# A recurrent scan on one core: expert products in half-precision parts, smaller blocks, a shorter lead and another order on VectorE

## Chip, core and metric

One Trainium2 chip, one of its cores. The metric is the device time of one execution in microseconds (us). TensorE (PE) has two clock levels, 1.2 and 2.4 GHz; a profile shows the granted one as a share of 2.4 GHz.

## What is computed

Four layers on x of shape 8 x 256 x 512. The change touches layer 1's expert part and layer 2's wide product, and the order of work in the scan that computes layers 1 and 2 together:

```python
# layer 1, conditioning: a GRU over 256 steps, state h of 8 x 512
r = sigmoid(i_r + h_r); z = sigmoid(i_z + h_z); n = tanh(i_n + r * h_n)
h = (1 - z) * n + z * h
# layer 1, experts, on every state h of the GRU
base_out = einsum('bsd,od->bso', x, W_base) + b_base
expert_idx = argmax(softmax(x @ router_W.T)); onehot = one_hot(expert_idx)
out = base_out + 2 * einsum('bser,eor->bso', (x @ A) * onehot, Bw)
# layer 2, conditioning: 256 Runge-Kutta steps (4 evaluations each)
dq = q - q**3/3 - p + drive + tanh(q) @ coupling.T + bias     # drive = layer 1's output at that step
dp = 0.08 * (q + 0.7 - 0.8 * p)
# layer 2, retrieval: hidden layer of 2048 on every state q
h = silu(q @ W_up.T + b_up);  h = h @ W_down.T + b_down        # then keys, top 8, gather by products
```

## The kernel before

Phases run one after the other, each closed by a barrier of all engines: attention and experts of layer 0, gates (`gates`, the GRU's input products), `scan`, `retrieve_experts`, attention and experts of layer 3.

**The scan.** The GRU runs LEAD = 29 steps ahead of the oscillator (the Runge-Kutta steps), since the drive of oscillator step t is the expert output for GRU state t. So there is a prologue of 29 GRU steps alone (first `for s in range(LEAD)` of every engine), then the loop over t = 0 to 255 in which oscillator step t and GRU step s = t + 29 are woven together, and from t = 227 on the oscillator is alone. Nothing plans the order: it is written out by hand for every engine, and each engine runs its list in order, with semaphores between them.

- *TensorE.* One evaluation k = 0..3 of a step (`evaluate`) is 16 products of 8 columns (L631, low part of the weights) and 16 of 16 columns (L634, high part with both parts of the state), all 128x128 f16 weights. Between evaluations lie the GRU's three gates R, N and Z in the same form (`gate_low`, `gate_high`), 96 products a step. At the end of a step comes a slice of the experts (`experts`), for blocks of TL = 16 steps, 128 columns of states, in f32: slices 0 and 1 the router and A product (L663), 2 to 9 the base product (L669), slice 4 also a transpose (L672), 10 and 11 the product with Bw (L676). So 12 of 16 steps carry a slice. In a profile an f32 product counts as two matmul records.
- *VectorE.* It sums the partial products (L863, "reduce" below; it ends each evaluation), makes the low part of tanh(q) for TensorE (`low_part`, L852), and the cubic term, the Runge-Kutta sums and the GRU's elementwise work. Its order in evaluation 0 is: G0 and Q, Z gate's first sum (`pre`, L763 into g_a), `low_part`, `arg`, cubic, Q1, `total`, then the GRU update (`upd`, `state_half` L802, `state_full` L806), then the reduce. After evaluation 3's reduce comes the clamp (L867). In slice 12 it adds bias and x to the expert output (L826, four instructions of 128x128) into XT.
- *ScalarE.* tanh(q) twice (L723 as f16, L724 as f32), the scaled copies (L726, L709), square, the gates' sigmoids and tanh.
- *GpSimd (POOL).* Per step the drive (L745, L747), L752, and the copy of q into HQ (L756).

**Retrieval.** For s = 0..7 (256 tokens each) TensorE runs `up` (L1006: 16 tiles m by 4 chunks, f32 weights 128x128, 256 columns, two PSUM banks in turn), `pairs`, `similar`, `down`; ScalarE empties the banks (`hidden`, L1108), VectorE does top 8. The weights wait in GRZ, loaded by DMA once the GRU has ended.

Of the kernel before, what the change touches and what calls it, by code (L numbers as in the profile page):

```python
# [573 lines left out]
LEAD, TL = 29, 16  # L574

def scan(nc, K, XT, GRZ, HQ, wm, whi, wlo, chi, clo, bhn, cond_d, bias_d, wb_d, bb_d, ar_d, bw_d, wup, wdn, wup_d, wdn_d, s_pw):

    with ExitStack() as c:
# [49 lines left out]
        def _(e):  # L628
# [1065 lines left out]
```

## Time and profile before

| | us |
|---|---|
| median of 3 runs | 5070.73 (5060.59 to 5075.04) |
| profiled execution | 5060.11 |
| its span | 5058.5 |
| TensorE busy | 4811.2 (95%) |
| VectorE busy | 2748.1 (54%) |
| ScalarE busy | 1687.5 (33%) |
| GpSimd busy | 357.5 (7%) |
| mean granted TensorE clock | 0.781 |

The scan takes the stretch from about 903 to 2899 us of the span, retrieval from 2901 to 4310. A busy share counts an instruction's whole duration, so overlapping ends of pipelined matmuls hide short gaps: in the scan a step is read better from the start times of its groups.

### The profile page before, as it was taken

What the parts mean: (1) busy time and instruction counts of PE and PEld (TensorE: products, weight loads), DVE (VectorE), ACT (ScalarE), POOL (GpSimd) and SP (SyncE); (2) the same over time, 40 slices, a digit from 0 to 9 for tenths busy, and PEclk for the clock granted to TensorE, in tenths of its full rate; (3) what the DMA queues carried; (4) which work ended last, traced back from release to release, by engine and by line L of the source; (5) the groups of instructions that cost most, each with busy time, mean ns of one, the idle gap of its engine ahead of it and who ended that gap; (6) DMA issues with size and microseconds to landing.
All of it is one profiled execution on the core that took longest, in us unless ns stands there. A gap on an engine that the chain in (4) does not pass through costs nothing. (4 is left out here: it accounts for less than half of the span.)

```text
span 5058.5 us, 197415 instructions
## 1 busy us (share of the span) xinstructions
PE 4811.2 (95%) x83680; PEld 3821.2 (76%) x83680; DVE 2748.1 (54%) x15134; ACT 1687.5 (33%) x7030; POOL 357.5 (7%) x1123
## 2 busy tenths in 40 slices
PE   8999989699999999999998699999999999999999
PEld 3335654699999999999997588789999999444444
DVE  3110020488888888888888726575553342344421
ACT  1101111245555555555554322233322221233320
POOL 1100010011111111111111100000000000000000
PEclk7999989555555555555555599999989999899999
DMA  3202330000000000000001000023320000100000
GB/s 106 106 10 111 150 124 8 16 4 5 5 5 5 5 5 5 5 5 5 5 5 53 13 9 2 33 71 94 92 77 3 3 3 2 47 8 8 10 7 33
DMA packets 52292, 159.62 MB, mean 32 GB/s; under 512 B 13873, under 2 KB 14001, under 8 KB 46272
## 3 DMA queue, kind: packets, MB, share of 16 engines
q1 hardware_dynamic: 45408, 130.70, 7.7%
q8 instruction: 651, 10.67, 0.9%
q0 software_dynamic: 3712, 12.29, 0.7%
q10 hardware_dynamic: 2304, 4.20, 0.2%
q14 instruction: 217, 1.78, 0.1%
HBM read 129.63 MB, written 17.17 MB: 29 GB/s over the span
## 5 line engine op out<-in xcount | busy, mean ns | idle before, releaser
L631 PE MATMUL k_ps<-k_hx,k_wlo 128*128 128x8 f16 x16384 | 604.9, 169 | 95.5 <-ACT k_hx L723 95.0
L631 PEld LDWEIGHTS k_ps<-k_hx,k_wlo 128*128 128x128 f16 x16384 | 545.7, 105 | 135.2 <-ACT k_hx L723 111.0
L634 PE MATMUL k_ps<-k_hl,k_whi 128*128 128x16 f16 x16384 | 590.0, 174 | 2.9 <-issue 0.4
L634 PEld LDWEIGHTS k_ps<-k_hl,k_whi 128*128 128x128 f16 x16384 | 519.4, 104 | 7.4 <-issue 1.8
L631 PE MATMUL g_ps<-g_hx,g_wlo 128*128 128x8 f16 x12288 | 434.2, 168 | 47.1 <-DVE g_hx L802 41.9
L634 PE MATMUL g_ps<-g_hl,g_whi 128*128 128x16 f16 x12288 | 436.9, 174 | 4.2 <-issue 4.1
L631 PEld LDWEIGHTS g_ps<-g_hx,g_wlo 128*128 128x128 f16 x12288 | 384.9, 104 | 59.0 <-DVE g_hx L802 52.3
L634 PEld LDWEIGHTS g_ps<-g_hl,g_whi 128*128 128x128 f16 x12288 | 385.1, 104 | 4.4 <-issue 4.4
L723 ACT ACTIVATE k_hx<-k_q 128x32 f16<-128x32 f32 x768 | 176.1, 229 | 567.1 <-DVE k_q L863 564.1
L1475 DVE TENSOR_REDUCE t_NM<-t_ps 128x1 f32<-128x512 f32 x256 | 165.0, 686 | 218.3 <-PE t_ps L1341 218.3
L863 DVE TENSOR_REDUCE k_q<-k_ps 128x32 f32<-128x96 f32 x768 | 196.8, 256 | 147.6 <-PE k_ps L634 122.0
L1246 DVE TENSOR_TENSOR HQ<-p_ior,p_pm 128x2048 f32<-128x2048 f32 x61 | 139.4, 2290 | 217.0 <-PE p_sim L1065 217.0
L490 DVE TENSOR_TENSOR m_hT<-GRZ,m_ps 128x256 f32<-128x256 f32 (+1 forms) x72 | 36.6, 508 | 383.5 <-ACT GRZ L453 377.4
L1075 PE MATMUL p_dn<-wm,GRZ 128*128 128x128 f32 x2048 | 241.4, 280 | 2.0 <-ACT wm L1133 2.0
L1075 PEld LDWEIGHTS p_dn<-wm,GRZ 128*128 128x128 f32 x2048 | 235.3, 195 | 3.4 <-ACT wm L1133 2.2
L1075 PE MATMUL p_pq<-r_mem,GRZ 128*128 128x128 f32 x2048 | 236.3, 276 | 0.0
L726 ACT ACTIVATE k_hl<-k_hx 128x32 f16<-128x32 f16 x1024 | 235.1, 230 | 0.0
L1075 PEld LDWEIGHTS p_pq<-r_mem,GRZ 128*128 128x128 f32 x2048 | 230.9, 192 | 1.1
L1006 PE MATMUL p_up<-HQ,GRZ 128*128 128x256 f32 x1024 | 225.2, 382 | 1.8 <-PEq L22 1.8
L1006 PEld LDWEIGHTS p_up<-HQ,GRZ 128*128 128x128 f32 x1024 | 196.5, 192 | 29.1 <-issue 1.9
L728 ACT ACTIVATE k_sq<-k_q 128x32 f32<-128x32 f32 x1024 | 218.1, 213 | 0.0
L852 DVE CUSTOM_DVE_ANT_0 k_hl<-k_T,k_hx 128x32 f16<-128x32 f32 x1024 | 191.1, 187 | 7.9 <-ACT k_T L724 0.2
(340 smaller groups left out, 8994.4 us busy)
## 6 DMA issues: line engine op xcount, KB each, us to landing
GRZ<-expert_places SPq DMA_DIRECT2D x64, 512.0 KB, 4.9
wm<-in_w_dram SPq DMA_DIRECT2D x4, 2816.0 KB, 10.2
GRZ<-in_w_dram SPq DMA_DIRECT2D x4, 2816.0 KB, 9.8
m_w<-in_w2a_dram SPq DMA_DIRECT2D x8, 1280.0 KB, 12.6
GRZ<-in_ue_dram SPq DMA_DIRECT2D x8, 1024.0 KB, 7.9
GRZ<-in_x_nat_dram SPq DMA_DIRECT2D x4, 1024.0 KB, 10.3
XT<-in_xT_dram SPq DMA_DIRECT2D x1, 4096.0 KB, 26.9
expert_rows<-wm SPq DMA_DIRECT2D x1, 4096.0 KB, 17.3
```

The costliest lines, as they stand in the source:

```text
L490: V.tensor_tensor(hT[0:M,m,0:n],sA[0:M,st,0:n],ps[st*2+1][0:M,0:n],ALU.mult).then_inc(s_h,1)
L631: T.matmul(P[:,1,j*NB:(j+1)*NB],lo[:,kc,(m0+j)*128:(m0+j+1)*128],x[:,kc,:],start=(j==0 and kc==0),stop=False,skip_group_check=True)
L634: i=T.matmul(P[:,:,j*NB:(j+1)*NB],hi[:,kc,(m0+j)*128:(m0+j+1)*128],x[:,kc,:,:],start=False,stop=kc==KC-1,skip_group_check=True)
L723: A.activation(kx[:],m4(src),ACT.Tanh,scale=uq[k]).then_inc(k_hi,1)
L726: A.activation(kl[:,:,0,:],kx[:],ACT.Copy,scale=S).then_inc(k_hS,1)
L728: A.activation(sq[:],q[:,k,:],ACT.Square,scale=uq[k]).then_inc(k_sq,1)
L852: V.tensor_tensor_reduce(kl[:,:,1,:],m4(Tt[:]),kx[:],S,0.0,ALU.subtract,ALU.max,lz[:,0:1]).then_inc(k_lo,1)
L863: V.tensor_reduce(qn[:] if k==3 else q[:,k+1,:],ksum(k),AX.X,ALU.add).then_inc(k_q,1)
L1006: x=T.matmul(psu[n%2][:,(m%2)*256:(m%2+1)*256],wup[:,dd,m*128:(m+1)*128],HQ[:,dd,s*256:(s+1)*256],start=dd==0,stop=dd==3)
L1075: x=T.matmul(pso[i%2][:,dd*128:(dd+1)*128],ue[:,cc,dd*128:(dd+1)*128],Ws[i%2][:,cc,:],start=cc==0 and dd==0,stop=cc==31,skip_group_check=True)
L1246: V.tensor_tensor(B0[q] if i==0 else Bp[:,q],bc(ior[:].unsqueeze(1),[128,16,128]),bc(PM[:,i,1,q*16:(q+1)*16].unsqueeze(2),[128,16,128]),AL ...
L1475: V.tensor_reduce(NM[:,qc,hh*64+32:hh*64+33],psX[hh][:,:],AX.X,ALU.max,negate=True).then_inc(s_mx,1)
```

## The change

1. Experts of the scan in f16: the weights (base and A with router) are scaled and split on GpSimd into a high and a low f16 part; each f32 product becomes three f16 products (high x high, high x low, low x high). The states are kept as f16 parts (HX, HL) written by the GRU's own instructions, in place of HS; the f32 state stays in HF for two steps. The product with Bw stays f32.
2. Blocks of TL = 8 steps (64 columns); slices at steps 0 to 6 of 8. LEAD = 17.
3. Expert output: ScalarE copies PSUM to `ex` (slice 7), GpSimd adds it to XT; the bias is added to XT beforehand on GpSimd. VectorE's four instructions (L826) are gone.
4. VectorE's order: the Z gate's `pre` and `arg` and the clamp (`limit`) come ahead of `low_part(t,0)`, then `diff` (before ahead of evaluation 3's reduce), G0, Q, `upd`, cubic, `state_half`, `total`, reduce; `state_full` and Q1 move into evaluation 1; `low_part` goes ahead of `low` and of `pre(s,R)` in evaluations 1 and 2.
5. q goes to HQ as two f16 parts: GpSimd runs three instructions a step (`state_out`) in place of one copy.
6. Retrieval's `up`: W_up is split into f16 parts at the start of the phase, in four rounds of one ScalarE copy and one VectorE instruction, 128x2048 each, and each product becomes three f16 products of 256 columns.

```diff
-LEAD, TL = 29, 16
+LEAD, TL = 17, 8
 # TensorE, experts
+                def base(u0,u1):
+                    for u in range(u0,u1):
+                        dc,d=u//4,u%4
+                        P=pso[:,dc*TN:(dc+1)*TN]; wh=wbh[:,d,dc*128:(dc+1)*128]; wl=wbl[:,d,dc*128:(dc+1)*128]
+                        T.matmul(P,wh,hS[:,d,:],start=u==0,stop=False,skip_group_check=True)
+                        T.matmul(P,wh,lS[:,d,:],start=False,stop=False,skip_group_check=True)
+                        T.matmul(P,wl,hx[:,d,:],start=False,stop=False,skip_group_check=True)
...
-                    for d in (2*i,2*i+1):
-                        x=T.matmul(psh[:,0:136],hs[:,d,:],ar[:,d,:],start=d==0,stop=d==3)
+                    for d in (2*i,2*i+1):
+                        T.matmul(psh[0:TN,0:136],hS[:,d,:],arh[:,d,:],start=d==0,stop=False)
+                        T.matmul(psh[0:TN,0:136],lS[:,d,:],arh[:,d,:],start=False,stop=False)
+                        x=T.matmul(psh[0:TN,0:136],hx[:,d,:],arl[:,d,:],start=False,stop=d==3)
+                    base(i,i+1)
+                if i==2: base(2,7)
+                if i==3:
+                    base(7,11)
+                    e.wait_ge(l_ht,j+1)
+                    T.transpose(pst[:,0:TN],ht[:],K.ident[0:TN,0:TN]).then_inc(l_tr,1)
+                if i==4: base(11,16)
+                if i in (5,6):
 # ScalarE, evaluation 1
+            def expert_out(s):
+                if i!=7 or j<0 or j>=NT//TL: return
+                e.wait_ge(l_o,j+1)
+                if j>0: e.wait_ge(l_x,j)
+                A.activation(ex[:].rearrange('p d t b -> p (d t b)'),pso[:,0:KC*TN],ACT.Copy,scale=US).then_inc(l_e,1)
 # GpSimd, ahead of its loop
+            e.wait_ge(s_lw,64)
+            G.tensor_scalar(both,both,SW,None,ALU.mult).then_inc(s_sp,1)
+            G.tensor_copy(high,both).then_inc(s_sp,1)
+            G.tensor_tensor(both,both,high,ALU.subtract).then_inc(s_sp,1)
+            G.tensor_scalar(low_,both,S,None,ALU.mult).then_inc(s_sp,1)
+            for dc in range(KC): G.tensor_scalar(XT[:,dc],XT[:,dc],bb[:,dc:dc+1],None,ALU.add).then_inc(s_bx,1)
 # GpSimd, in its loop
-                    G.tensor_copy(HQ[:,:,:,t-1],m4(q[:,0,:])).then_inc(k_out,1)
+                    state_out(t-1)
+                results(t+LEAD)
 # VectorE, evaluation 0
+                if t>0:
+                    pre(s-1,Z_)
+                    limit(t-1)
+                    arg(s-1,Z_)
+                low_part(t,0)
+                if t>0: diff(s-1)
                 e.wait_ge(k_q0,t+1)
                 n_G=ch.did(stt(G0[:],p[:],-BETA*6/h,q[:,0,:]))
                 e.wait_ge(k_u,t+1)
                 n_Q=ch.did(stt(Q[:,0,:],q[:,0,:],1/3,E0[:]))
-                if t>0: pre(s-1,Z_)
-                low_part(t,0)
-                if t>0: arg(s-1,Z_)
+                if t>0: upd(s-1)
                 cubic(t,0)
-                n_Q1=ch.did(stt(Q[:,1,:],G0[:],-a*EPS*h/6,Q[:,0,:]))
+                if t>0: state_half(s-1)
                 total(t,0,Q[:,0,:],n_Q)
-                if t>0: upd(s-1); state_half(s-1); state_full(s-1)
                 end(t,0)
+                if t>0: state_full(s-1)
 # retrieval
-                        x=T.matmul(psu[n%2][:,(m%2)*256:(m%2+1)*256],wup[:,dd,m*128:(m+1)*128],HQ[:,dd,s*256:(s+1)*256],start=dd==0,stop=dd==3)
+                        T.matmul(P,wh,qh,start=dd==0,stop=False)
+                        T.matmul(P,wh,ql,start=False,stop=False)
+                        x=T.matmul(P,wl,qh,start=False,stop=dd==3)
...
+            for x in range(4):
+                if x>0: e.wait_ge(s_wl,x)
+                A.activation(wpair(x)[:,:,0,:],wup[:,:,x*512:(x+1)*512],ACT.Copy,scale=SW).then_inc(s_wh,1)
...
+            for x in range(4):
+                e.wait_ge(s_wh,x+1)
+                V.scalar_tensor_tensor(wpair(x)[:,:,1,:],wup[:,:,x*512:(x+1)*512],SW,wpair(x)[:,:,0,:],ALU.mult,ALU.subtract).then_inc(s_wl,1)
```

## Rows read from the trace of the kernel before

**Rows 1.** Busy time by stretch: from:to, length, PE, PEld, DVE, ACT, POOL, clock, DMA.

```profile
1033.00:2700.00 1667.00, 1624.84 (x51403) 1584.93 (x51404) 1450.52 (x11206) 843.09 (x5224) 222.45 (x904) 0.50 0.02 5
...
3040.00:3240.00 200.00, 197.03 (x924) 160.19 (x923) 119.05 (x743) 54.97 (x104) 0.00 (x0) 1.00 0.01 2
```

**Rows 2.** PE timeline, a step without experts: start, us, engine, line, count, idle before.

```profile
1268.14 0.59 PE L631 MATMUL k_ps<-k_hx,k_wlo 128*128 128x8 f16 x16 [0.25 <-ACT k_hx L723]
1268.75 0.57 PE L634 MATMUL k_ps<-k_hl,k_whi 128*128 128x16 f16 x16
...
1270.15 0.57 PE L631 MATMUL k_ps<-k_hx,k_wlo 128*128 128x8 f16 x16
1270.58 0.57 PE L634 MATMUL k_ps<-k_hl,k_whi 128*128 128x16 f16 x16
...
1271.77 0.59 PE L631 MATMUL k_ps<-k_hx,k_wlo 128*128 128x8 f16 x16
...
1273.92 0.57 PE L634 MATMUL k_ps<-k_hl,k_whi 128*128 128x16 f16 x16
...
1275.18 0.59 PE L631 MATMUL k_ps<-k_hx,k_wlo 128*128 128x8 f16 x16 [0.25 <-ACT k_hx L723]
```

**Rows 3.** PE timeline, a step that ends with an expert slice.

```profile
1244.78 1.20 PE L669 MATMUL l_pso<-g_HS,wm 128*128 128x128 f32 x4
1245.77 0.61 PE L631 MATMUL k_ps<-k_hx,k_wlo 128*128 128x8 f16 x16
...
1253.07 0.61 PE L631 MATMUL k_ps<-k_hx,k_wlo 128*128 128x8 f16 x16
```

**Rows 4.** Timeline of all engines from one step's last reduce to evaluation 0's.

```profile
1046.68 0.25 DVE L863 TENSOR_REDUCE k_qn<-k_ps 128x32 f32<-128x96 f32 x1
...
1047.36 0.24 POOL L756 COPY HQ<-k_q 128x32 f32<-128x32 f32 x1
...
1047.53 0.18 DVE L852 CUSTOM_DVE_ANT_0 k_hl<-k_T,k_hx 128x32 f16<-128x32 f32 x1
...
1048.35 0.19 DVE L802 TENSOR_TENSOR g_hx<-g_m,g_n 128x32 f16<-128x32 f32 x1
...
1048.56 0.25 DVE L863 TENSOR_REDUCE k_q<-k_ps 128x32 f32<-128x96 f32 x1
```

**Rows 5.** Bounds of the scan's stages: two prologue steps, the oscillator's first and last, t = 227, L826.

```profile
942.19 1.02 PE L631 MATMUL g_ps<-g_hx,g_wlo 128*128 128x8 f16 x32 [1.58 <-DVE g_hx L802]
...
946.50 1.01 PE L631 MATMUL g_ps<-g_hx,g_wlo 128*128 128x8 f16 x32 [1.58 <-DVE g_hx L802]
...
L631 PE MATMUL k_ps<-k_hx,k_wlo x16384: 167/168/214, 1033.4 to 2898.4; 128*128 128x8 f16 x200
...
2704.05 0.59 PE L631 MATMUL k_ps<-k_hx,k_wlo 128*128 128x8 f16 x16 [0.25 <-ACT k_hx L723]
...
1264.50 1.46 DVE L826 SCALAR_TENSOR_TENSOR XT<-l_pso,l_bb,XT 128x128 f32<-128x128 f32 x4
```

**Rows 6.** PE timeline of retrieval, `up` of two rounds.

```profile
3047.36 27.79 PE L1006 MATMUL p_up<-HQ,GRZ 128*128 128x256 f32 x128
...
3097.68 12.68 PE L1006 MATMUL p_up<-HQ,GRZ 128*128 128x256 f32 x58
```

**Rows 7.** Groups by line and shape: engine, shapes, count, busy us, mean ns, idle before.

```profile
L459 ACT ACTIVATE GRZ<-m_ps 128x512 f32<-128x512 f32 x8 | 4.7, 592 | 0.0
...
L568 DVE SCALAR_TENSOR_TENSOR g_wc<-g_wc,g_whi 128x2048 f32<-128x2048 f32 x3 | 6.9, 2292 | 0.1
...
L1108 ACT ACT_TABLE_LOAD x13 | 16.7, 1283 | 9.3 <-PE p_up L1006 9.1
```

**Rows 8.** GpSimd prices, and a VectorE instruction beside one of GpSimd's in layer 0.

```profile
L225 POOL MEMSET a_RS<- 128x1024 f32 x1 | 1.0, 951 | 0.0
...
29.63 4.50 POOL L231 TENSOR_TENSOR a_wor<-a_wor 16x2048 f32<-16x2048 f32 x1
32.73 1.68 DVE L246 TENSOR_SCALAR a_CB<-a_cm,a_pc 128x512 f32<-128x512 f32 x1
```

More of the change, by code:

```diff
@@ L640, in gate_low @@
                 if x==R_ and j0==0: e.wait_ge(g_hi,s+1)
-                for j in range(j0,j1): products_low(gsum(x),wlo,hx,x*4,j)
+                for j in range(j0,j1): products_low(gsum(x),wlo,hxs(s),x*4,j)
             def gate_high(s,x,j0,j1):
@@ L644, in gate_high @@
                 if x==R_ and j0==0: e.wait_ge(g_lo,s+1)
-                for j in range(j0,j1): i=products_high(gsum(x),whi,hl,x*4,j)
+                for j in range(j0,j1): i=products_high(gsum(x),whi,lambda kc: hls(s)[:,:,kc,:],x*4,j)
                 if j1==KC: i.then_inc(g_mm[x],1)
@@ L651, in evaluate @@
                 e.wait_ge(k_lo,t*4+k+1)
-                for j in range(KC): i=products_high(kout[k%2],chi,kl,0,j)
+                for j in range(KC): i=products_high(kout[k%2],chi,lambda kc: kl[:,kc,:,:],0,j)
                 i.then_inc(k_mm,1)
@@ L735, in _ @@
                         scaled(s)
-                    elif k==1: masked(s)
+                    elif k==1: masked(s); expert_out(s)
                     elif k==2: sig_r(s)
@@ L747, in drive, with results, state_out @@
                 G.tensor_scalar(Ds[:],D[:],1/US,None,ALU.mult).then_inc(k_Ds,1)
+            def results(s):
+                j,i=s//TL-1,s%TL
+                if i!=7 or j<0 or j>=NT//TL: return
+                e.wait_ge(l_e,j+1)
+                x=XT[:,:,:,j*TL:(j+1)*TL].rearrange('p d b t -> p d t b')
+                G.tensor_tensor(x,ex[:],x,ALU.add).then_inc(l_x,1)
+            e.wait_ge(s_lw,64)
+            both=wm[:,0:2592]; high,low_=split[:,0:2592],split[:,2592:5184]
+            G.tensor_scalar(both,both,SW,None,ALU.mult).then_inc(s_sp,1)
+            e.wait_ge(s_sp,1)
+            G.tensor_copy(high,both).then_inc(s_sp,1)
+            e.wait_ge(s_sp,2)
+            G.tensor_tensor(both,both,high,ALU.subtract).then_inc(s_sp,1)
+            e.wait_ge(s_sp,3)
+            G.tensor_scalar(low_,both,S,None,ALU.mult).then_inc(s_sp,1)
+            for dc in range(KC): G.tensor_scalar(XT[:,dc],XT[:,dc],bb[:,dc:dc+1],None,ALU.add).then_inc(s_bx,1)
+            def state_out(t):
+                if t>0: e.wait_ge(k_ol,t)
+                G.tensor_scalar(qs[:],q[:,0,:],uq[0]*SQ,None,ALU.mult).then_inc(k_out,1)
+                e.wait_ge(k_out,t+1)
+                G.tensor_copy(HP[:,:,:,t,0],m4(qs[:])).then_inc(k_oh,1)
+                e.wait_ge(k_oh,t+1)
+                G.tensor_tensor(HP[:,:,:,t,1],m4(qs[:]),HP[:,:,:,t,0],ALU.subtract).then_inc(k_ol,1)
             e.wait_ge(s_i,5)
+            e.wait_ge(s_bx,4)
+            for s in range(LEAD): results(s)
             drive(0)
@@ L886, in _ @@
                 n_C=ch.did(stt(B0[:,1,:],G0[:],cD,AQ[:,1,:]))
+                low_part(t,1)
+                n_Q1=ch.did(stt(Q[:,1,:],G0[:],-a*EPS*h/6,Q[:,0,:]))
                 low(s)
-                low_part(t,1)
                 ch.after(n_B)
@@ L903, in _ @@
                 n_W=ch.did(stt(W[:,1,:],q[:,1,:],a*hh*(2-2*kap+2*kap*kap),W[:,0,:]))
+                low_part(t,2)
                 pre(s,R_)
-                low_part(t,2)
                 arg(s,R_)
```

103 lines of the change are left out of this document (52 added, 51 removed).

## Prediction, written before the change was run

> **What bounds the kernel now.** I read busy time by stretch first. In the scan [rows 1] TensorE is busy 97% of the time at a granted clock of 0.50 (1.2 GHz), VectorE 87%; in retrieval's first part TensorE 98.5% at 1.00 and VectorE 60%. The second is simply TensorE-bound. The first needs the timeline, since busy time there hides short gaps.
>
> *A step without experts* [rows 2] takes 1275.18 - 1268.14 = 7.04 us. One evaluation that nothing disturbs goes from its first product (1270.15) over its high products (1270.58, 0.43 later) to the next evaluation's first (1271.77, 1.19 later): 1.62. That is a closed chain, products, reduce, tanh, products; the gate products lie in its pauses. Four such make 6.48, so 0.56 of the step is waiting. Evaluation 0 holds most: 0.61 and 1.40 in place of 0.43 and 1.19. [Rows 4] show why: `low_part` starts 0.85 after the last reduce, behind four other instructions, and the high products wait for it; then the GRU update sits ahead of the reduce, which starts only at 1.88; and the half-precision state (L802, 1.67) comes late, so that the gate products start late and evaluation 1 behind them (0.11). Evaluation 2 loses 0.09 behind `pre(s,R)`, evaluation 3 loses 0.07 (1.26 for 1.19) behind `diff`.
>
> *A step with an expert slice* [rows 3] takes 7.30, and here TensorE is the bound at the step's end: the slice lasts 0.99, evaluation 0 starts when it ends. 7.30 - 0.99 = 6.31 is what such a step costs beside its slice. I write the slice as X: step = 6.31 + X.
>
> The whole woven part goes from 1033.4 to 2704.05 [rows 5]: 1670.7 for 227 steps, 7.36 each. The pattern alone (12 slices, L826 once, which makes a step of about 7.77 by holding the reduce for its 1.46) gives 7.30, so 0.06 is irregular. The prologue's step is 4.31 (946.50 - 942.19), and the oscillator alone takes 195 for 29 steps, 6.72 each.
>
> **The change, part by part.**
>
> *Lead.* 12 prologue steps go: 12 x 4.31 = -51.7. In the prologue slices hide in the 1.58 that TensorE waits for the state. 12 steps move from "oscillator alone" to "woven".
>
> *Order on VectorE.* In evaluation 0 `low_part` has three instructions ahead of it now, but the first, the Z gate's `pre`, waits for the last gate products (an estimate: 32 products at 0.027 and 0.15 for the last one's end, 1.0 after 1273.92 in [rows 2], some 0.4 after the reduce). I get: `pre` 0.44, clamp 0.55, `arg` 0.66, `low_part` 0.77 (before 0.85), reduce at 1.69 (before 1.88), half state at 1.41 (before 1.67). With evaluation 1's 0.11, evaluation 2's 0.09 and evaluation 3's 0.07 a step without experts goes to about 6.52. `state_full` and Q1 fall into evaluation 1, where VectorE waits for TensorE ahead of the reduce; by [rows 1] an instruction holds it for at most 1450.5 / 11206 = 0.13, and I take it that two just fit. If that cover is gone, each costs its 0.1. In a slice step TensorE hides evaluation 0's disorder already; left is the 0.09 of evaluation 2: 6.22 + X.
>
> *Slices.* An f32 record of 128 columns took 0.248 (0.99 / 4) for two passes, 0.124 a pass. A 64-column pass at 1.2 GHz is then between 64/1.2 = 0.053 and 0.062 if the weight load hides; sixteen f16 pairs of load and product of 8 columns fit into 0.43 [rows 2], 0.027 each. Above, if it doesn't hide, 0.08 to 0.085. I take 0.055. Fifteen of them (slices 2, 4) are 0.82; slices 0 and 1 (six of 136 columns, three of 64) 0.86; slice 3 with its transpose 0.81; slices 5 and 6 stay f32 with the same weights, so up to 0.99. Mean of seven: X = 0.88. Seven of eight steps carry one, where it was twelve of sixteen. Average: (7 x 7.10 + 6.52) / 8 = 7.03, plus 0.06 irregular and 0.02 for the router's small instructions, which come twice as often: 7.11. ScalarE's `expert_out` and GpSimd's addition fall once in 8 steps, in evaluation 1, on engines that are 51% and 13% busy in the scan [rows 1]; behind `expert_out` stands evaluation 2's tanh, due over 1 us later, behind the addition only the next step's work: 0. L826 is gone, which the pattern has (its lack is worth 0.73 in 16 steps). Woven part: 239 x 7.11 = 1699 against 1671: +28.6.
>
> *Oscillator alone.* 17 x 6.53 + 0.8 for the last block's slices = 111.8 against 195: -83.2.
>
> *GpSimd in the prologue.* Once the weights land it runs four instructions of 2592 elements and four of 2048. [Rows 8] price one without a second input at 0.95 per 1024, one with two at 4.50 per 2048: about 3 x 2.35 + 5.7 + 4 x 1.9 = 20.4 in all, 41 if all go at the upper price. It is done before TensorE's first slice (step 8, over 30 us in), so no engine waits for the result. But [rows 8] show a VectorE instruction (L246, else 0.54) that took 1.68 and ended 0.3 after the GpSimd instruction it met. Of the GRU's eleven VectorE instructions most read two operands from SBUF. If each that meets GpSimd waits so, the prologue stands almost still for those 20 us; if only L246's kind is held, nothing is lost. Bounds 0 and 41; I take 15, nearer to the row that shows a hold, less what TensorE does meanwhile. The Trainium skill, page SBUF — State Buffer, section Who interferes with whom, says that a VectorE instruction with two SBUF inputs contends with a GpSimd instruction that reads SBUF, and that the holder keeps the port for its whole instruction: by that rule the term would be some 20, without it 0. For L246 the trace agrees; for two SBUF inputs no row of size decides it, and the short pairs in the scan, `low_part` at 0.18 inside L756 [rows 4], show no lengthening.
>
> *Two more GpSimd instructions a step* (`state_out`): GpSimd is 13% busy [rows 1] and nothing waits for them in the loop (the clamp waits for the first of them a step later): 0; at the scan's end three instructions of about 0.25 in place of one, 0.7 with their waits.
>
> *Retrieval.* `up` took 27.79 for 64 f32 products [rows 6], 0.434 each or 0.109 a pass of 256 columns. Three passes: 192 x 0.109 = 20.8, -7.0 a round, -56 in eight. Bounds: 256/2.4 = 0.107, and 0.109 + 0.027 if the load of weights doesn't hide (-1.6 a round). VectorE (30 us of a round of 50.3, then 43.3) stays covered. *Its start* costs: ScalarE's copy of 2048 is about 1.8 (four times L459 less its fixed part; 2.4 at most), VectorE's 2.29 [rows 7], and the rounds wait for each other: 4.2 a round. TensorE starts 4.2 later and fills two banks, then waits for ScalarE, which is free only after its fourth copy and a table load, at about 16.4. It has then done 5.3 of the 14.7 it would have done, and falls back to the low clock once more: +11.
>
> **Sum:** -51.7 + 28.6 - 83.2 + 15 + 0.7 - 56 + 11 = -135.6. The profiled execution took 5060.1, giving 4924.5; it lies 10.6 below the median of the runs, so on the median's scale 4935.
>
> **Rivals.**
>
> *A wait takes the place of the one removed (0.17).* VectorE works in order, and `pre(s-1,Z)` now stands ahead of the clamp and `low_part`, waiting for TensorE's last gate group. For it: VectorE is 87% busy, and evaluation 1 has no spare slot left. Against: by the estimate above the Z group ends 0.4 after the reduce, early enough for `low_part` at 0.77. Then a step without experts stays 7.04 and one with a slice 6.31 + 0.88: 7.25 on average, 33 more, with the tail's 2: 4970.
>
> *All cheaper (0.12).* No hold in the prologue (-15), and f32 slices of 64 columns at nearer half (X = 0.80, -17): 4900.
>
> *Half precision isn't cheaper here (0.07).* If the weight load doesn't hide behind 64 columns, X = 1.25: 0.37 x 7/8 x 239 = 77 more, 5012; the change would do its arithmetic and not save it. Against: 8 and 16 columns took the same 0.027.
>
> *Slower (0.04).* The hold of [rows 8] in every step: GpSimd now runs six instructions of about 0.25 in a step and three fall into evaluation 0's crowded stretch. If VectorE waits 0.25 for each of the three, 0.8 a step, 239 steps add 190 and the time is 5125. It beats the rest of the change from 0.57 a step. The same rule of the Trainium skill speaks for it. Against it: `low_part` inside GpSimd's copy keeps its 0.18 [rows 4].
>
> **From this to the numbers.** The forecast has 0.60. The range takes in the first two rivals and the port's bounds: 4875 to 5000; it leaves out the last two. About 0.3% (15 us, the spread of the three runs) can be told from no change. All but the slower rival lie below that: faster 0.95, same 0.01, slower 0.04.
>
> **What would show it.** Steps of 6.5 and 7.1 in TensorE's timeline; `low_part` under 0.8 after the reduce; 64-column products 0.055 apart; prologue steps around 910 to 930 us stretched beside GpSimd's large instructions; `up` rounds of 20.8 and a first one with a gap of some 5 us; clock still 0.50 in the scan. Steps of 7.25, or 0.08 apart in the slices, would make it wrong.

## The result, and the profile after

The changed kernel took 5016.28 us (median of 4 runs, 5001.09 to 5026.26) against 5065.66 for the kernel before (4 runs, 5055.51 to 5075.04): ratio 0.9904, 95% interval 0.9881 to 0.9926. That is faster by 49 us, 1%, and clear of the runs' noise; the forecast was 4935 in 4875 to 5000, so the sign was right and the size was not. The profiled execution took 5001.09 us with a span of 4998.4, the shortest of the four runs.

Busy time by stage of the changed kernel (from:to, length, then PE, PEld, DVE, ACT, POOL, clock, DMA share, GB/s): the prologue, the 239 woven steps, the oscillator alone, and retrieval up to its first gather product.

```profile
901.20:1006.80 105.60, 54.70 (x1711) 51.58 (x1712) 66.75 (x208) 16.04 (x72) 44.99 (x14) 0.50 0.04 14
1006.80:2770.20 1763.40, 1726.69 (x55598) 1668.93 (x55599) 1515.88 (x11826) 896.77 (x5558) 469.94 (x1461) 0.50 0.02 5
2770.20:2883.70 113.50, 75.18 (x2245) 68.93 (x2245) 88.31 (x641) 48.02 (x326) 29.94 (x99) 0.50 0.15 59
2883.70:3277.30 393.60, 373.41 (x2520) 295.95 (x2521) 232.69 (x1379) 120.29 (x215) 1.29 (x5) 0.98 0.07 24
```

TensorE is still the busiest, at 98% of the woven part (97% in [rows 1]), and the clock is 0.50 there as before. So the busy shares don't show the difference; the lengths do. From the start times in both traces (the stages are bounded by the first gate product, the oscillator's first tanh, its tanh at step 256 - LEAD, its last product and the first product of the gather):

| stage | before | after | moved | forecast |
|---|---|---|---|---|
| up to the scan | 903.05 | 901.24 | -1.8 | 0 |
| prologue | 130.05 (29 steps) | 105.25 (17) | -24.8 | -36.7 |
| woven | 1670.67 (227 steps, 7.360) | 1763.39 (239, 7.378) | +92.7 | +28.6 |
| oscillator alone | 195.24 (29) | 113.44 (17) | -81.8 | -83.2 |
| scan's end to first gather | 429.4 | 394.0 | -35.4 | -44.3 |
| the rest | 1730.1 | 1721.1 | -9.0 | 0 |
| sum | 5058.5 | 4998.4 | -60.1 | -135.6 |

Three terms are off: the woven part by 64 us, the prologue by 12, retrieval (the row from the scan's end to the first gather) by 9. The rest of the table is unchanged code, and its -9.0 and -1.8 belong to no edit: in the runs below, the stage ahead of the scan ended between 901 and 923 and the last one took 1718 to 1730, whatever the kernel did in between. So I compare stages below, not spans; the scan's stages repeat far more closely (woven part 1763.4 and 1764.7 in two executions of the changed kernel).

**The prologue.** The timeline where GpSimd's first large instruction runs (start, duration, engine, line, operation):

```profile
906.58 6.78 POOL L779 TENSOR_SCALAR wm<-wm 128x2592 f32<-128x2592 f32 x1 [188.13 <-DMA l_bb<-in_bb_dram]
...
907.40 0.25 DVE L822 TENSOR_REDUCE g_hn<-g_ps 128x32 f32<-128x96 f32 x1
...
907.78 4.70 DVE L834 TENSOR_TENSOR g_t<-g_r,g_hn 128x32 f32<-128x32 f32 x1
912.52 0.21 DVE L812 SCALAR_TENSOR_TENSOR g_w<-g_t,HQ 128x32 f32<-128x32 f32 x1
...
913.42 2.34 POOL L781 CAST wm<-wm 128x2592 f16<-128x2592 f32 x1
...
913.85 1.96 DVE L846 TENSOR_TENSOR g_m<-g_z,g_d 128x32 f32<-128x32 f32 x1 [0.29 <-ACT g_z L720]
915.85 0.19 DVE L850 TENSOR_TENSOR g_HX<-g_m,g_n 128x32 f16<-128x32 f32 x1
915.85 5.14 POOL L783 TENSOR_TENSOR wm<-wm 128x2592 f32<-128x2592 f32 x1
915.96 5.08 DVE L854 TENSOR_TENSOR g_HF<-g_m,g_n 128x32 f32<-128x32 f32 x1
```

A 0.19 us VectorE instruction lasts 4.70, 1.96 and 5.08 beside GpSimd, each time one that reads both operands from SBUF; the sum over PSUM at 907.40 keeps its 0.25. Eight instructions were held in this way, for 28 us in all beyond their 0.19. The last two of those shown end with GpSimd's instruction. The first does not: it ends at 912.48, and the next instruction, at 912.52, reads two SBUF tiles and keeps 0.21, while L779 is recorded until 913.36. Beside the other `tensor_scalar` instructions it is the same: the hold ended 0.9 us (L785) and 1.7 us (each of the four bias additions, L786) before the recorded end. Whether these held the port for less than their length, or their ends are recorded late, is not shown. This is the hold that I had put at 15 us.

**A step.** The intervals between the tanh (L746) of one evaluation and of the next, mean us over steps 16 to 235 by the step's place in its block of 8. The slice of the experts that stands at the end of the previous step falls into evaluation 0. "e3" to "e10" are kernels of the next section.

| slice ahead | eval. 0 | 1 | 2 | 3 | step | e3 | e8 | e10 |
|---|---|---|---|---|---|---|---|---|
| none | 1.85 | 1.73 | 1.68 | 1.65 | 6.92 | 7.11 | 6.94 | 6.84 |
| 0 | 2.35 | 1.73 | 1.65 | 1.67 | 7.40 | 7.38 | 7.36 | 7.35 |
| 1 | 2.35 | 1.73 | 1.87 | 1.66 | 7.60 | 7.38 | 7.51 | 7.31 |
| 2 | 2.07 | 1.72 | 2.00 | 1.67 | 7.46 | 7.33 | 7.40 | 7.14 |
| 3 | 2.32 | 1.73 | 1.65 | 1.67 | 7.37 | 7.35 | 7.31 | 7.36 |
| 4 | 2.07 | 1.73 | 1.69 | 1.65 | 7.14 | 7.21 | 7.11 | 7.10 |
| 5 | 2.20 | 1.72 | 1.67 | 1.65 | 7.24 | 7.23 | 7.18 | 7.17 |
| 6 | 2.21 | 2.38 | 1.67 | 1.65 | 7.91 | 7.61 | 7.84 | 7.49 |

The kernel before has 1.88, 1.74, 1.71, 1.70 in a step without a slice and 2.26, 1.63, 1.71, 1.70 in an ordinary one with a slice (medians). Three things stand out: evaluation 1 is 1.72 in every place but the last, where it was 1.63 in a step with a slice; evaluation 2 is longer in two places (the router's instructions on VectorE); evaluation 1 is 2.38 in the last place. Of that last one the timeline:

```profile
1288.97 0.36 ACT L736 ACTIVATE l_ex<-l_pso 128x256 f32<-128x256 f32 x1
...
1289.42 0.87 POOL L776 TENSOR_TENSOR XT<-l_ex,XT 128x256 f32<-128x256 f32 x1 [1.35 <-ACT l_ex L736]
1289.47 0.86 DVE L812 SCALAR_TENSOR_TENSOR k_Q<-k_q,k_K 128x32 f32<-128x32 f32 x1
...
1290.25 0.18 DVE L812 SCALAR_TENSOR_TENSOR k_ps<-k_g,k_Q 128x32 f32<-128x32 f32 x1
1290.35 0.18 DVE L812 SCALAR_TENSOR_TENSOR k_W<-k_q,k_AP 128x32 f32<-128x32 f32 x1
1290.54 0.26 DVE L905 TENSOR_REDUCE k_q<-k_ps 128x32 f32<-128x96 f32 x1
```

The same hold, now inside the loop: GpSimd's addition of 256 columns, 0.87 us, and a VectorE instruction of 0.86 in its shadow. I had costed this addition at nothing, since GpSimd is idle and nobody waits for its result.

**Retrieval's start.** ScalarE's and VectorE's rounds over the weights, and TensorE behind them:

```profile
2886.04 1.91 ACT L1192 ACTIVATE wm<-GRZ 128x2048 f16<-128x2048 f32 x1 [3.42 <-PEq L22]
...
2887.99 2.29 DVE L1318 SCALAR_TENSOR_TENSOR wm<-GRZ,wm 128x2048 f16<-128x2048 f32 x1 [4.15 <-ACT wm L1192]
2890.31 1.91 ACT L1192 ACTIVATE GRZ<-GRZ 128x2048 f16<-128x2048 f32 x1 [2.36 <-DVE wm L1318]
2890.42 0.37 PE L1059 MATMUL p_up<-HQ,wm 128*128 128x256 f16 x1 [7.10 <-DVE wm L1318]
```

As forecast, 4.2 us a round (1.91 and 2.29); TensorE begins 7.10 after the scan's end where it was 1.82, and waits once more, 4.9 us, for ScalarE's L1163. At the full clock products stand 0.113 apart.

### The profile page after: what moved, and what is told of

It reads as the page before. It is cut to its first block and busy times, and to the rows that moved or that the text cites. A ratio compares the mean times of both kernels' runs of the same rounds, so it can differ in the third digit from the quotient of the medians.

```text
span 4998.4 us, 202235 instructions
## 1 busy us (share of the span) xinstructions
PE 4763.3 (95%) x85616; PEld 3762.8 (75%) x85616; DVE 2759.2 (55%) x15139; ACT 1702.6 (34%) x7083; POOL 651.4 (13%) x1675
## 3 DMA queue, kind: packets, MB, share of 16 engines
q14 instruction: 224, 1.84, 0.1%
## 5 line engine op out<-in xcount | busy, mean ns | idle before, releaser
L639 PE MATMUL g_ps<-g_HX,g_wlo 128*128 128x8 f16 x12240 | 433.1, 168 | 33.6 <-DVE g_HX L850 33.3
L642 PE MATMUL g_ps<-g_HL,g_whi 128*128 128x16 f16 x12240 | 437.0, 174 | 12.5 <-DVE g_HL L818 12.5
L639 PEld LDWEIGHTS g_ps<-g_HX,g_wlo 128*128 128x128 f16 x12240 | 384.3, 104 | 38.2 <-DVE g_HX L850 35.3
L642 PEld LDWEIGHTS g_ps<-g_HL,g_whi 128*128 128x128 f16 x12240 | 384.5, 104 | 12.8 <-DVE g_HL L818 12.7
L746 ACT ACTIVATE k_hx<-k_q 128x32 f16<-128x32 f32 x768 | 176.1, 229 | 593.8 <-DVE k_q L905 593.8
L800 POOL TENSOR_TENSOR k_E<-k_Ds,k_p 128x32 f32<-128x32 f32 x256 | 64.3, 251 | 1227.8 <-DVE k_p L971 1227.7
L1488 ACT ACTIVATE t_PT<-t_ps 128x512 f32<-128x512 f32 x256 | 138.9, 595 | 155.1 <-PE t_ps L1425 150.5
```

What stands on the lines that cost most here:

```text
L639: T.matmul(P[:,1,j*NB:(j+1)*NB],lo[:,kc,(m0+j)*128:(m0+j+1)*128],x[:,kc,:],start=(j==0 and kc==0),stop=False,skip_group_check=True)
L746: A.activation(kx[:],m4(src),ACT.Tanh,scale=uq[k]).then_inc(k_hi,1)
L800: G.tensor_tensor(E0[:],Ds[:],p[:],ALU.subtract).then_inc(k_u,1)
L1488: A.activation(PT[:,kc,hh,:],psE[hh][:,:],ACT.Exp).then_inc(s_e,1)
```

## The experiments

All but the last three are single executions, so their stages are read, not their times. How far to trust a stage is seen where nothing in it was edited: the woven part repeats within 3 us (e5, e11), the prologue within 0.4, but for e2, where it is 5 us shorter: its first step took 4.1 us, otherwise some 8. The stages, in us:

| kernel | prologue | woven | alone | scan's end to gather |
|---|---|---|---|---|
| changed | 105.25 | 1763.4 | 113.4 | 394.0 |
| e1, results cut | 105.4 | 1750.1 | 112.9 | 393.8 |
| e2, W later | 100.3 | 1764.1 | 113.2 | 393.8 |
| e3, old order | 105.1 | 1750.5 | 113.4 | 393.7 |
| e4, f32 `up` | 105.4 | 1763.6 | 113.3 | 428.6 |
| e5, split cut | 83.1 | 1766.4 | 113.5 | 393.4 |
| e6, router spread | 105.5 | 1750.8 | 113.1 | 393.5 |
| e8, sum first | 105.25 | 1751.6 | 113.1 | 394.2 |
| e9, f32 experts | 89.9 | 1919.7 | 118.4 | 392.7 |
| e10, mended | 82.8 | 1726.6 | 113.0 | 393.0 |
| e11, changed again | 105.4 | 1764.7 | 113.3 | 393.1 |
| e12, results on VectorE | 86.3 | 1723.3 | 112.6 | 394.4 |

**e1: GpSimd's addition in eight pieces.**

```diff
-G.tensor_tensor(x,ex[:],x,ALU.add).then_inc(l_x,1)
+for dc in range(KC):
+    for u in range(2):      # four steps of one chunk: 32 columns
+        x=XT[:,dc,:,j*TL+u*4:j*TL+u*4+4].rearrange('p b t -> p t b')
+        i_=G.tensor_tensor(x,ex[:,dc,u*4:u*4+4,:],x,ALU.add)
+i_.then_inc(l_x,1)
```

> Only GpSimd's `results` differs: its one addition of 256 columns per block becomes eight of 32 columns (one block of the state each), in the same place of its queue. In the changed kernel evaluation 1 of the step that holds it takes 2.38 us from one ScalarE tanh to the next where the others take 1.72, and a VectorE instruction beside the 0.87 us addition takes 0.85. Theory A (one long GpSimd instruction that reads SBUF keeps a VectorE instruction with two SBUF inputs waiting until it is over): with instructions of 0.26 us the longest VectorE one falls from 0.85 to below 0.35, evaluation 1 of that step falls to 1.75 to 1.95, and the 239 woven steps lose 30 x 0.45 to 0.63, 13 to 19 us. Rival (the 0.36 us copy of the experts' sum on ScalarE, or GpSimd's total work, is what delays the evaluation): evaluation 1 stays at 2.3 or above, as GpSimd's work grows, and the woven steps gain less than 3 us.

Measured: woven part -13.3 us; evaluation 1 of that place 1.81 (2.38), its evaluation 2 1.78 (1.67). GpSimd was busy longer with it (61.0 us in the whole kernel instead of 28.0), and the loss shrank. So it is the length of one GpSimd instruction that counts, not their sum: theory A. ScalarE's copy, the rival, was unchanged. Of the 0.66 a block, 0.2 stays, which the pieces still cost.

**e2: the last VectorE instruction of evaluation 1 moved behind its sum.**

```diff
-e.wait_ge(k_ap,t+1)
-n_W=ch.did(stt(W[:,0,:],q[:,0,:],...,AP[:]))
 end(t,1)
+e.wait_ge(k_ap,t+1)
+n_W=ch.did(stt(W[:,0,:],q[:,0,:],...,AP[:]))
```

> One VectorE instruction (the recovery variable's first partial sum W, 0.18 us, one every 0.10 us of the queue) moves from the end of evaluation 1, ahead of its sum, to the beginning of evaluation 2, where VectorE waits some 0.15 us for ScalarE. Theory B (VectorE's queue is what ends last in evaluation 1): evaluation 1 falls from 1.72 to 1.63 us, evaluation 2 stays at 1.65, the woven steps lose 239 x 0.09 = 21 us. Rival (TensorE and ScalarE set evaluation 1, VectorE is only near them): no interval moves by more than 0.02 and the woven steps by less than 5 us. A third way: evaluation 2 takes up what evaluation 1 loses (1.65 to 1.74), and the sum stays.

Measured: nothing; evaluation 1 stays at 1.72. Theory B as I had put it falls. VectorE's timeline of evaluation 1 in e2, its first row `low_part`, its last the sum:

```profile
1320.85 0.19 DVE L894 CUSTOM_DVE_ANT_0 k_hl<-k_T,k_hx 128x32 f16<-128x32 f32 x1
...
1321.48 0.18 DVE L812 SCALAR_TENSOR_TENSOR k_Q<-k_q,k_K 128x32 f32<-128x32 f32 x1
1321.59 0.20 DVE L812 SCALAR_TENSOR_TENSOR k_ps<-k_g,k_Q 128x32 f32<-128x32 f32 x1
1321.90 0.26 DVE L905 TENSOR_REDUCE k_q<-k_ps 128x32 f32<-128x96 f32 x1
```

With nothing in between, the reduce starts 0.31 after the start of the partial sum (`total`) whose result it adds. In the changed kernel, with W between them, it is 0.30 (1297.10 to 1297.40). The time from `total` to the reduce covers W, which is free there; what stands ahead of `total` is not. (e6 has two instructions there, and the same 0.30.)

**e3: VectorE's order of before, the rest as changed.**

> VectorE's order of a step is put back to that of the kernel before (clamp straight after the sum of evaluation 3, the difference h-n before that sum, the reset of Q, the full state in evaluation 0); everything else of the change stays. It gives the price of the reorder alone. My prediction had it at 0.52 us per step without experts (7.04 to 6.52) and little on a step with a slice that fills TensorE. Theory B (the reorder moved VectorE's queue from between the steps into evaluations 0 and 1, so it gained less): a step without a slice goes from 6.92 (changed kernel) to 7.04 to 7.10, steps with a slice rise by 0.05 to 0.12, the woven part by 12 to 28 us. Rival (the reorder gained what was forecast, and slices or GpSimd took it back): the woven part rises by more than 60 us.

Measured: the woven part is 12.9 us *shorter* with the old order. Neither theory had that. The same stretch of VectorE's timeline in e3:

```profile
1315.63 0.19 DVE L894 CUSTOM_DVE_ANT_0 k_hl<-k_T,k_hx 128x32 f16<-128x32 f32 x1
...
1316.05 0.18 DVE L812 SCALAR_TENSOR_TENSOR k_Q<-k_q,k_K 128x32 f32<-128x32 f32 x1
1316.17 0.20 DVE L812 SCALAR_TENSOR_TENSOR k_ps<-k_g,k_Q 128x32 f32<-128x32 f32 x1
1316.28 0.18 DVE L812 SCALAR_TENSOR_TENSOR k_W<-k_q,k_AP 128x32 f32<-128x32 f32 x1
1316.59 0.26 DVE L905 TENSOR_REDUCE k_q<-k_ps 128x32 f32<-128x96 f32 x1
```

`total` starts 0.54 after `low_part`, in the new order 0.74: Q1 and `low(s)` have come in between. In e3 the reduce waits 0.42 after `total`, that is, for TensorE; in the new order it waits for `total`. That Q1 and `low(s)` are the ones is read from these lines; no run moved these two alone. The table of steps shows the rest. Ahead of a slice the new order shortens evaluation 3 (1.70 to 1.64), and evaluation 0 behind it grows by as much (2.30 to 2.36 by medians), since between them TensorE is the bound. The new order gains 0.06 in evaluation 2 of an ordinary step and 0.19 in the step without a slice. It loses 0.09 in evaluation 1 behind slices 0, 1, 3 and 5; behind the short slices 2 and 4 the old order is at 1.71 too (medians). And it makes the router's instructions dearer: in e3 evaluation 2 is 1.72 and 1.84 with them and 1.71 without, in the changed kernel 1.87 and 1.99 against 1.65, since there `total` starts 1.06 after the tanh and in e3 0.91. So `total` is late in evaluation 2 as well, and no experiment put it earlier there. The new order also raises what GpSimd's addition costs: in e3 that evaluation takes 2.10, 0.46 more than its neighbours, in the changed kernel 2.38, 0.66 more, for there the held instruction stands ahead of `total` and in e3 behind it.

**e4: retrieval's wide layer in single precision again, one GpSimd instruction for three.**

```diff
-G.tensor_scalar(qs[:],q[:,0,:],uq[0]*SQ,None,ALU.mult)
-G.tensor_copy(HP[:,:,:,t,0],m4(qs[:]))
-G.tensor_tensor(HP[:,:,:,t,1],m4(qs[:]),HP[:,:,:,t,0],ALU.subtract)
+G.tensor_copy(HQ[:,:,:,t],m4(q[:,0,:]))
...
-T.matmul(P,wh,qh,...); T.matmul(P,wh,ql,...); x=T.matmul(P,wl,qh,...)
+x=T.matmul(P,wup[:,dd,m*128:(m+1)*128],HQ[:,dd,s*256:(s+1)*256],...)
```

> Retrieval's wide layer goes back to single precision (no halves of its weights, one product instead of three), and with it GpSimd's state output in the scan back to one copy instead of three instructions. It gives the price of that part alone, and whether the two extra GpSimd instructions per step cost the scan. Theory A (only long GpSimd instructions hold VectorE; 32-column ones don't): the woven part moves by less than 5 us, retrieval from the scan's end to the first gather takes 30 to 40 us more (429 against 394). Rival (GpSimd's short instructions hold VectorE too, in each step): the woven part gets 239 x 0.1 = 24 us or more faster, and that is the greater part of what the prediction missed.

Measured: woven part 1763.6 against 1763.4, though GpSimd is busy 276.6 us of it instead of 469.9; retrieval 34.6 us longer. The two GpSimd instructions of 32 columns that e4 takes out of each step's six had cost the loop nothing that shows; in the changed kernel VectorE's instructions in evaluation 0 beside them take 0.18 to 0.22. What the other four cost was not tried. The wide layer is worth 35 us.

**e5: GpSimd's prologue instructions in pieces of at most 128 columns.**

```diff
-G.tensor_scalar(both,both,SW,None,ALU.mult).then_inc(s_sp,1)
+for x in C_: i_=G.tensor_scalar(both[:,x],both[:,x],SW,None,ALU.mult)   # 21 slices
+i_.then_inc(s_sp,1)
...
```

> GpSimd's eight large instructions of the prologue (four of 2592 columns that split the experts' weights, four of 2048 that add their bias) become 84 and 64 of at most 128 columns, same place, same work. In the changed kernel the prologue takes 105.3 us from the first gate product to the first oscillator tanh; 17 steps of 4.31 us and the 5.2 around them would be 78.5. Theory A (a VectorE instruction with two SBUF inputs waits for the end of GpSimd's instruction): it then waits at most 0.4 us at a time; the prologue falls to 78 to 90, the longest VectorE instruction in it from about 5 us to under 0.6. Rival (the port is lost for the sum of GpSimd's work, however it is cut, 43 us of it and more with the cuts): the prologue stays above 100.

Measured: prologue 83.1 (105.3), although GpSimd is busy 73.9 us of it instead of 45.0. VectorE beside the first 21 pieces:

```profile
914.98 10.21 POOL L780 TENSOR_SCALAR wm<-wm 128x128 f32<-128x128 f32 x21 [188.50 <-DMA l_bb<-in_bb_dram]
...
918.47 0.35 DVE L862 TENSOR_TENSOR g_HF<-g_m,g_n 128x32 f32<-128x32 f32 x1
918.92 0.39 DVE L826 SCALAR_TENSOR_TENSOR g_HL<-g_HF,g_HL 128x32 f16<-128x32 f32 x1
920.88 0.41 DVE L842 TENSOR_TENSOR g_t<-g_r,g_hn 128x32 f32<-128x32 f32 x1
```

0.35 to 0.41 in place of up to 5.08. Theory A again; 22 us for loops around eight instructions.

**e6: the router's four VectorE instructions one by one.**

```diff
-elif i==2:
+elif i==2 and part==1:
...
 total(t,2,Q[:,2,:],n_Q2)
 n_W=...
-experts(s,0); experts(s,1)
+experts(s,0)
 end(t,2)
...
 total(t,3,X[:,3,:],n_X)
+experts(s,1)
 end(t,3)
```

> VectorE's four expert instructions of a block, now two at the end of evaluation 2 in each of two steps, stand one by one at the ends of evaluations 2 and 3 of those steps. In the changed kernel they lengthen evaluation 2 of these steps from 1.65 to 1.87 and 1.99 us, 0.56 per block. Theory B (an evaluation's sum starts 0.29 us after the start of VectorE's last partial sum, in whose shadow an instruction or two cost nothing, and only what is more is late): evaluation 2 goes to 1.65 to 1.75 in both steps, evaluation 3 to 1.64 to 1.80, the woven part gains 29 x 0.35 to 0.5, 10 to 15 us. Rival (each expert instruction costs its own time wherever it stands): no gain, within 3 us.

Measured: evaluation 2 is 1.65 (median) in both places, evaluation 3 1.64 and 1.65, the woven part -12.6 us. In the changed kernel both stand behind `total` and W, and the second needs the first's result: it starts 0.19 later, where others follow at 0.10, and the reduce behind it comes 0.54 after `total`:

```profile
1491.17 0.20 DVE L812 SCALAR_TENSOR_TENSOR k_ps<-k_g,k_Q 128x32 f32<-128x32 f32 x1
1491.28 0.18 DVE L812 SCALAR_TENSOR_TENSOR k_W<-k_q,k_W 128x32 f32<-128x32 f32 x1
1491.38 0.15 DVE L860 TENSOR_REDUCE l_mx<-l_psh 64x1 f32<-64x8 f32 x1
1491.57 0.22 DVE L863 SCALAR_TENSOR_TENSOR l_mk<-l_psh,l_mx,l_io 64x8 f32<-64x8 f32 x1
1491.71 0.24 DVE L905 TENSOR_REDUCE k_q<-k_ps 128x32 f32<-128x96 f32 x1
```

The gain can come from the room behind `total` or from no longer waiting for the partner; e6 doesn't tell the two apart. In e6 even the 0.33 us instruction of 128 columns fits:

```profile
1335.12 0.19 DVE L812 SCALAR_TENSOR_TENSOR k_ps<-k_g,k_X 128x32 f32<-128x32 f32 x1
1335.22 0.33 DVE L869 SCALAR_TENSOR_TENSOR l_ht<-l_io,l_ix,l_psh 64x128 f32<-64x128 f32 x1
1335.48 0.24 DVE L905 TENSOR_REDUCE k_qn<-k_ps 128x32 f32<-128x96 f32 x1
```

**e8: the partial sum ahead of what doesn't end the evaluation.**

```diff
-if t>0: state_half(s-1)
 total(t,0,Q[:,0,:],n_Q)
+if t>0: state_half(s-1)
...
-n_X=...(X[:,0,:],Q[:,0,:],B0[:,1,:]...)
 cubic(t,1)
-n_Q2=...(Q[:,2,:],q[:,1,:],...)
+n_X=...(X[:,0,:],Q[:,0,:],B0[:,1,:]...)
 total(t,1,Q[:,1,:],n_Q1)
+n_Q2=...(Q[:,2,:],q[:,1,:],...)
```

> VectorE's order as changed, but in evaluation 0 the partial sum (total) goes ahead of the half-precision state, and in evaluation 1 ahead of X and the Q for evaluation 2, which then stand in the 0.29 us between it and the sum. The last run showed that the instruction behind the partial sum is not what ends evaluation 1: the sum starts 0.30 after the start of the partial sum in both orders. Theory B, mended (the partial sum's own start is late: 1.13 us after the tanh, against 0.92 in the old order, where TensorE ended last): partial sum at 0.92 to 1.0, evaluation 1 from 1.72 to 1.63 to 1.65, in the step without a slice evaluation 0 from 1.85 to 1.75, the woven part 239 x 0.08 = 17 to 23 us faster. Rival (the sum is late for another reason, ScalarE's or TensorE's order): evaluation 1 stays at 1.72, the woven part within 4 us.

Measured: evaluation 1 is 1.63 (median) in steps with a slice, as forecast (1.75 in the step without one, where it was 1.72, and 2.28 in the last place); evaluation 0 of the step without a slice stays at 1.85, since `total` there waits for the cubic term. By medians of the intervals the woven part has 18.2 us less, in the sum 11.8: 6.5 more of short irregular stalls (last section).

**e9: the experts in single precision, with blocks of 8.**

> The experts' base and selection products go back to single precision (one product instead of three), with blocks of 8 steps, lead 17 and everything else of the change kept; the split of their weights in the prologue goes too, GpSimd's bias additions stay. Price of the half-precision parts alone. From the rows: a 64-column product in single precision takes 0.22 us apart against 3 x 0.054 = 0.16 for its three parts, a 136-column one 0.45 to 0.48 against 3 x 0.113 = 0.34. Forecast: slices of 1.12, 1.12, 1.10, 0.88, 1.10 us instead of 0.84, 0.84, 0.80, 0.64, 0.80, that is 29 blocks x 1.4 = 41 us more in the woven part, and 15 us less in the prologue. Rival (the slices hide behind VectorE, so their price matters little): the woven part within 15 us.

Measured: woven part +156 us, prologue -15. My expectation misread the records: a 64-column f32 product leaves two, 0.22 apart each, so it costs 0.44, not 0.22. Slice 3 of e9, its four products and their end:

```profile
1351.80 1.95 PE L669 MATMUL l_pso<-g_HF,wm 128*128 128x64 f32 x8
1353.67 0.37 PE L683 MATMUL l_pst<-ident,l_ht 64*128 64x64 f32 x1
```

Four products in 1.87 (0.47 each); with 128 columns a product takes 0.99 / 2 = 0.50 [rows 3]. Halving the columns of an f32 product saves almost nothing, so blocks of half the length have twice the expert work. The three f16 products of 64 columns cost 0.16 together. The half-precision parts are worth 156 us in the woven part, less 15 for their split in the prologue, and are what pays for the short blocks.

**e10: the four mends together** (in evaluation 0 also the cubic term ahead of Q), and **e11**, the changed kernel beside it, in the same rounds.

> The four edits that each run alone has priced, together: GpSimd's results in eight pieces, its prologue instructions in pieces of at most 128 columns, VectorE's expert instructions spread over evaluations 2 and 3, partial sums ahead of what does not end an evaluation (in evaluation 0 also the cubic term ahead of Q). If they add up, since each takes a wait from another evaluation of the step: woven part 1763.4 - 13.3 - 12.6 - 11.8 = 1726 us, by the medians of the intervals 49 less, 1714; prologue 83; scan 1982 - 59 to 71 = 1911 to 1923; the kernel some 65 us below the changed one, 4935 to 4965 us, ratio to the kernel before 0.975 to 0.981. If they share a wait, the woven part stays above 1735.

> The changed kernel once more, unaltered, on the same chip and in the same rounds as the mended one, as its measure: ratio to the kernel before 0.988 to 0.993, scan 1982 us.

Measured: 4957.94 us (6 runs, 4943.35 to 4965.24), ratio to the kernel before 0.9784, interval 0.9758 to 0.9809. The changed kernel in the same rounds: 5011.04 (6 runs), 0.9902, interval 0.9877 to 0.9927. So the mends are worth another 53 us, as much as the whole change. Stages of e10, as above:

```profile
918.00:1000.80 82.80, 54.30 (x1710) 51.33 (x1710) 44.99 (x208) 15.73 (x69) 74.76 (x161) 0.50 0.05 17
1000.80:2727.40 1726.60, 1706.94 (x55597) 1662.15 (x55597) 1495.63 (x11825) 897.18 (x5556) 489.52 (x1670) 0.50 0.02 5
```

The woven part lost 36.8; the three runs alone add up to 13.3 + 12.6 + 11.8 = 37.7. What GpSimd's pieces still cost is seen in the last place of the block:

```profile
1278.24 1.64 POOL L778 TENSOR_TENSOR XT<-l_ex,XT 128x32 f32<-128x32 f32 x7 [1.42 <-ACT l_ex L736]
1278.31 0.26 DVE L823 SCALAR_TENSOR_TENSOR k_ps<-k_g,k_Q 128x32 f32<-128x32 f32 x1
1278.48 0.30 DVE L823 SCALAR_TENSOR_TENSOR k_Q<-k_q,k_K 128x32 f32<-128x32 f32 x1
1278.71 0.30 DVE L823 SCALAR_TENSOR_TENSOR k_W<-k_q,k_AP 128x32 f32<-128x32 f32 x1
```

0.30 for 0.18: two VectorE instructions with both operands in SBUF are held for part of a piece each.

**e12: the experts' sum on VectorE again, otherwise e10.**

```diff
+elif i==7:
...
+    for dc in (2*part,2*part+1):
+        x=XT[:,dc,:,j*TL:(j+1)*TL].rearrange('p b t -> p t b')
+        V.scalar_tensor_tensor(x,pso[:,dc*TN:(dc+1)*TN]...,US,x,ALU.mult,ALU.add).then_inc(l_x,1)
```

> The mended kernel, but the experts' sum goes onto the state on VectorE again, as before the change: four instructions of 64 columns that read the accumulators directly, two at the end of evaluation 2 and two at the end of evaluation 3 of the same step; ScalarE's copy and GpSimd's eight additions go. It tells what the move of this work to GpSimd was worth. In the mended kernel it costs 0.29 in evaluation 1 and 0.13 in evaluation 2 of one step in eight, 0.42 per block. Theory C (VectorE has a free slot or so behind each partial sum; two instructions of 0.25 to 0.3 from the accumulators take one more): evaluations 2 and 3 take 0.1 to 0.25 more each, 0.2 to 0.5 per block, the woven part within 5 us of the mended one's 1726.6. Rival (what VectorE did itself is dear, as the single line of the kernel before that held the reduce for over 1 us in a step): 1.0 per block, 17 us more.

Measured: 4958.17 us (4 runs), ratio 0.9794, interval 0.9769 to 0.9820; woven part 1723.3. In the last place evaluation 2 takes 1.89 and evaluation 3 1.74 (medians), evaluation 1 its 1.63. By means that is 0.35 a block. The pieces on GpSimd cost 0.35 a block too: in e10 evaluation 2 takes 1.79 there, and evaluation 1 1.76 in half the blocks and 1.92 in the others (the 0.29 of the expectation holds for the second half only). There is nothing between the two. The move of this work to GpSimd, one of the change's aims, was worth nothing when both are done well, and as it was done it cost 0.66 a block.

## Why the prediction was wrong

**Woven part, forecast 7.11 a step, measured 7.378: 64 us.** By its own steps:

- *"I take it that two just fit"* (`state_full` and Q1 in evaluation 1). This is the step that failed. I asked whether VectorE is through when TensorE is, and bounded an instruction by its mean of 0.13. What ends the evaluation is the partial sum's start plus 0.30. Q1 and `low(s)` stand ahead of it, `total` is 0.20 later than in the old order, and 0.09 of that shows: 239 x 0.085 = 20 us. e3 and e8 show it from both sides, e2 shows where it isn't. (`state_full`, the other of the two, did fit: it runs while VectorE waits for the tanh.)
- *Evaluation 2 gives back 0.09*, from 1.71 to 1.62. It gave 0.06: the reduce comes 0.30 after `total` here too. 239 x 0.03 = 7 us.
- *`results` on GpSimd at nothing: "behind the addition only the next step's work".* 0.66 a block, 30 blocks, 20 us; e1 takes 13 of them away. I looked at who waits for the result, and not at what the instruction holds while it runs.
- *The router's instructions, 0.02 a step.* 0.22 and 0.35 in evaluation 2, 29 x 0.57 = 16 us, forecast 5: another 11 (e6). They come twice as often with blocks of half the length, and each block pays anew; and 0.15 of each of the two is the late `total` of evaluation 2 (e3 has 0.01 and 0.13).
- *Evaluation 0 without experts.* `pre` came 0.43 after the reduce, the clamp 0.54, `arg` 0.66, `low_part` 0.77, the half state 1.44: as forecast (0.44, 0.55, 0.66, 0.77, 1.41). The next reduce came at 1.84 instead of 1.69, again 0.29 after a late `total` (1295.38, 1295.67). Once in eight steps, so 4 us.
- *Slices.* 64-column f16 products were 0.05 apart (forecast 0.055). Taking the f32 slices of 0.88 as the measure, the seven average 0.90 (forecast 0.88): the router's products come to 1.03 (forecast 0.86), since TensorE pauses between them and the base products; the base slices of 15 products to 0.75. 5 us.

These are 67 us. I had allowed 0.06 a step for irregular stalls, of which 0.03 was there, 8 us less; so some 5 of the 64 I can't assign.

**Prologue, forecast +15 for the hold, measured 27** (105.3 against 29 steps' 130.05 less 51.7). The mechanism was right and the size off. GpSimd's eight instructions took 42.7 us in all, my upper price for them (41), not 20.4: the instructions that rescale (L779, L785) took 6.8 us for 2592 columns, 2.7 per 1024 where I had taken a MEMSET's 0.95. VectorE was held for 28 of the 42.7, since it is not always at an instruction with two SBUF inputs. The prediction cited the Trainium skill, page SBUF — State Buffer, section Who interferes with whom, for such a hold. The trace agrees on the hold: 4.70 and 5.08 for instructions with two SBUF inputs, 0.25 beside them for one that reads PSUM. It also showed that a GpSimd instruction with one input holds as one with two does (L781, 1.96). That the hold lasts for the whole instruction the trace confirms for L781 and L783; beside L779, L785 and L786 it ended 0.9 to 1.7 us earlier than their records do.

**The slower rival (0.04)** was this hold in every step. e4, and the 0.18 to 0.22 of VectorE's instructions in evaluation 0, exclude it for 32 columns at a time spread over a step; 32-column pieces one right after the other do hold (0.30 for 0.18 in e10), and 256 columns at once hold for 0.87. So the length of the one instruction decides.

**"A wait takes the place of the one removed" (0.17)** had the right kind of event in the wrong place. I named `pre(s-1,Z)`, ahead of the clamp, and it was on time; the new wait is for `total`. The time it gave, 4970, lay nearer, but for no reason of its own: it had no term for `results`, and none for the prologue beyond the 15.

**Retrieval, forecast -56 and +11, measured -35.** The rounds' first products came 44.4 apart where it had been 50.3: -5.9 each for the seven later rounds, since a pass took 0.113 instead of 0.109. The first round gained nothing: its `up` took 31.6 against 30.7. In it lie the 4.9 us wait and the lower clock, granted at 0.66 up to 2900 and 0.83 up to 2920, where before it was 0.76 up to 2915 and 1.00 from there. I had given this round the same -7 as the others and +11 for the start; it came to +1 for the round and +5 for the start.

**The lead and the oscillator alone** came as worked out: 12 steps of 4.31 (e5's prologue is within 5 us of it), 113.4 against 111.8.

## What to carry to other kernels

In a chain that closes through one instruction (here the reduce), look for the producers of its inputs and count back from each: producer's start plus latency. Instructions within that latency are free; instructions ahead of the producer delay it, and cost time as soon as it is what the chain waits for, whatever the engine's busy share is. So put the producer as early as its own inputs allow, and fill in behind it. Before work is moved to an idle GpSimd, ask how long its longest single instruction is, not how much there is; cut it, and VectorE passes in between (22 us in the prologue, 13 in the loop). And when a block is halved, list what is paid per block, a product whose cost hardly depends on its columns among it.

## What was not expected of the hardware

- An f32 product of 64 columns took 0.44 to 0.47 us at the 1.2 GHz level and one of 128 columns 0.50; three f16 products of 64 columns 0.16.
- From the start of VectorE's partial sum into PSUM to the start of the reduce that reads it passed 0.29 to 0.31 us wherever TensorE was done, with none, one or two instructions between them.
- Some 30 intervals of the woven part are 0.15 to 0.37 us longer than the others of their place, 8 us in all in the changed kernel. 20 of the 33 recur at the same steps in e1, e2, e4, e5, e6 and e11 (step 39, evaluation 2: 0.35 each time; step 5, evaluation 3: 0.31), so most hang on the program and not on chance. In e10 there are 68, 18 us. What they are was not tried.
